# Projected queries and keys kept whole in their slot, split in place during the value products; every row maximum taken for both heads at once

## The reference

```python
h = _ln(x, g1, be1)
x = _attn(h, h, Wq1, Wk1, Wv1, Wo1, bo1) + x          # self-attention, 1024 keys
h = _ln(x, g2, be2)
x = _attn(h, context, Wq2, Wk2, Wv2, Wo2, bo2) + x    # attention to 64 context rows
h = _ln(x, g3, be3)
y = h @ Wp + bp
x = y[..., :1024] * gelu(y[..., 1024:]) @ W2 + b2 + x

def _attn(x, ctx, Wq, Wk, Wv, Wo, bo):                # 16 heads of 64
    sim = einsum('bihd,bjhd->bhij', q, k) * 64 ** -0.5
    return einsum('bhij,bjhd->bihd', softmax(sim), v) @ Wo + bo
```

## Time and profile before

| what | us |
|---|---|
| median of 3 runs | 1986.89 (1986.82 to 1987.51) |
| the profiled execution, its own time | 1987.43 |
| its span in the profile | 1985.6 |
| PE busy | 1973.7 (99%) |
| POOL busy | 1490.1 (75%) |
| DVE busy | 1396.3 (70%) |
| ACT busy | 1143.7 (58%) |
| granted TensorE clock | 1.00 |

### The profile page before, as it was taken

How to read it: one execution, slowest core, us unless ns; L and a number is a source line. 1 busy time by engine, 2 the same in 40 slices (tenths; PEclk the granted TensorE clock), 3 DMA queues, 4 the chain that set the end, 5 groups by cost and what they waited for, 6 DMA issues and landing times.

```text
span 1985.6 us, 32165 instructions
## 1 busy us (share of the span) xinstructions
PE 1973.7 (99%) x12056; PEld 1353.4 (68%) x12056; DVE 1396.3 (70%) x2437; ACT 1143.7 (58%) x2042; POOL 1490.1 (75%) x800
## 2 busy tenths in 40 slices
PE   9999999999999999999999999999999999999999
PEld 7655655666565656755655666565569999888888
DVE  6688687666868886587787666867867888744443
ACT  6665576555656666465666555656756766533332
POOL 3699899989999998899899899989996665200000
PEclk9999999999999999999999999999999999999999
DMA  7201000001000000010000001000030420000000
GB/s 256 107 28 43 6 6 17 6 27 49 17 12 6 17 6 27 8 58 6 6 22 6 27 1 54 7 27 1 23 106 22 150 65 1 1 22 33 33 11 32
DMA packets 48956, 67.15 MB, mean 34 GB/s; under 512 B 6177, under 2 KB 42145, under 8 KB 46753
## 3 DMA queue, kind: packets, MB, share of 16 engines
q1 hardware_dynamic: 48800, 65.10, 10.2%
HBM read 45.17 MB, written 19.92 MB: 33 GB/s over the span
## 4 chain that ended last, share of the span: by engine, by line
PE 94%; POOL 3%; DVE 2%; issue 1%; ACT 1%; POOLq 0%; DVEq 0%
PE score L576 22%; PE score L555 19%; PE score L702 9%; PE attn_project L511 8%; PE attn_project L687 5%; PE attn_project L716 5%; PE score L523 5%; PE score L657 4%; PE score L625 3%; PE first_score L537 3%; PE attn_project L537 3%; PE score L561 3%; POOL acc L1545 2%; PE first_score L671 1%; PE first_score L587 1%
## 5 line engine op out<-in xcount | busy, mean ns | idle before, releaser
L1545 POOL TENSOR_TENSOR acc<-acc,pT 128x1024 f32<-128x1024 f32 x384 | 918.1, 2391 | 54.7 <-POOL acc L1545 1.4
L1289 ACT ACTIVATE pT<-score 128x1024 f32<-128x1024 f32 x512 | 507.7, 1027 | 107.5 <-PE score L561 70.4
L555 PE MATMUL score<-qk 64*128 64x512 f32 x3072 | 466.5, 405 | 0.9 <-ACT pT L1289 0.4
L576 PE MATMUL score<-pT,vT 128*64 128x512 f32 x1952 | 432.3, 595 | 0.0
L555 PEld LDWEIGHTS score<-qk 64*128 64x128 f32 x3072 | 269.0, 184 | 123.3 <-ACT pT L1289 82.0
L914 DVE TENSOR_REDUCE nmax<-attn_project 128x2 f32<-128x1024 f32 x256 | 312.7, 1221 | 7.3 <-PE attn_project L537 3.9
L576 PEld LDWEIGHTS score<-pT,vT 128*64 128x64 f32 x1952 | 134.8, 137 | 265.8 <-issue 243.8
L914 DVE TENSOR_REDUCE nmax<-first_score 128x2 f32<-128x1024 f32 x201 | 245.1, 1219 | 0.2 <-issue 0.2
L511 PE MATMUL attn_project<-hT,wqk 128*128 128x512 f32 x738 | 185.9, 400 | 0.0
L702 PE MATMUL score<-hT,wp 128*128 128x512 f32 x768 | 183.7, 395 | 0.0
L1542 POOL TENSOR_TENSOR acc<-pT 128x1024 f32<-128x1024 f32 x64 | 153.0, 2390 | 27.5 <-ACT pT L1289 27.5
(11 more groups left out here) (202 smaller groups left out, 3127.5 us busy)
## 6 DMA issues: line engine op xcount, KB each, us to landing
xres<-x_middle SPq DMA_DIRECT2D x10, 512.0 KB, 3.6
raw_qk<-in_L_xattn_Wq SPq DMA_DIRECT2D x32, 128.0 KB, 2.2
raw_qk<-in_L_xattn_Wk SPq DMA_DIRECT2D x32, 128.0 KB, 2.4
raw_v<-in_L_xattn_Wv SPq DMA_DIRECT2D x8, 512.0 KB, 4.7
keys_all<-keys SPq DMA_DIRECT2D x1, 4096.0 KB, 13.1
values_all<-values SPq DMA_DIRECT2D x1, 4096.0 KB, 13.3
out_x<-xres SPq DMA_DIRECT2D x7, 512.0 KB, 2.9
xres<-in_x SPq DMA_DIRECT2D x3, 1024.0 KB, 5.7
```

The source lines that it names most:

```text
L555: last = e.matmul(bank, key_part(P, h, r, jt), queries1[P % 2][r, w, c * BANK:(c + 1) * BANK], start=(fresh and part == 0), stop=(not fres ...
L576: last = e.matmul(banks[bank][head * DH:(head + 1) * DH, :], vT[:, v_slot(D, jt), c0:c0 + DH], pT[:, jt, head, :], start=(jt == 0), stop=( ...
L1289: e.activation(pT[:, jt].rearrange("p h n -> p (h n)"), SC[R % 2][:, :], ACT.Exp).then_inc(s.exponential, 1)
L1545: e.tensor_tensor(total, total, pT[:, jt], ALU.add).then_inc(s.probs_added, 1)
```

## The change

- ScalarE copies the projected keys and the scaled queries in full precision into the places that their lo parts will take (`keys_whole`, `queries_whole`: the same bytes as keys lo and queries lo), and rounds the keys for the first scores. With this the bank is free (`qk_kept`).
- The rest is done one pass later, during the value products, from SBUF to SBUF: VectorE changes the keys in place and takes one lo half (`change_keys`), ScalarE rounds the changed half and the queries, VectorE takes the other lo half and the queries' lo part (`split_qk`).
- `row_max_of`, `early_max` and `keys_full` are gone; all row maxima are taken for both heads at once.
- TensorE's two first scores of round 0 come after the scores of that round and not ahead of them.

```diff
-        keys_full = sb("keys_full", [PART, BANK // 2])
+        queries_whole = [tile[:, N:2 * N] for tile in (qk0_whole, qk1_whole)]
+        keys_whole = [tile[:, 2 * N:3 * N].rearrange("p (c n) -> p c n", c=CHUNKS) for tile in (qk0_whole, qk1_whole)]
...
+        def units(C):
+            after, c = C // CHUNKS + 1 + C % CHUNKS, C % CHUNKS
+            return [(after, 1 - c), (after, 3 - c)] if after < B * PAIRS else []
...
 # tensor
-                free[bank] = ((s.split_lo, qk_of[P, u]),)
+                free[bank] = ((s.qk_kept, qk_of[P, u]),)
...
             for C in range(NC):
-                if C + 1 < NC:
-                    for head in range(2):
-                        first_score(*next_part(C + 1, 0), head)
                 for jt in range(TILES):
...
-                    if C + 1 < NC and jt:
+                    if C + 1 < NC:
                         for head in range(2):
                             first_score(*next_part(C + 1, jt), head)
...
 # vector
-            def change_keys(P, u, bank, coming=None):
-                n, later = keys_of[P, u], banks[bank][:, PAIR:]
-                need.wait_ge(s.keys_rounded, n)
-                need.wait_ge(s.keys_copied, n)
-                e.tensor_tensor(keys_lo[P % 2][:, u, 0:PAIR], banks[bank][:, 0:PAIR],
+            def change_keys(P, u):
+                whole = keys_whole[P % 2][:, u, :]
+                need.wait_ge(s.qk_kept, qk_of[P, u])
+                e.tensor_tensor(whole[:, PAIR:], whole[:, PAIR:], whole[:, 0:PAIR], ALU.subtract
+                                ).then_inc(s.keys_changed, 1)
+                need.wait_ge(s.keys_changed, keys_of[P, u])
+                e.tensor_tensor(keys_lo[P % 2][:, u, 0:PAIR], whole[:, 0:PAIR],
                                 keys_hi[P % 2][:, u, PAIR:2 * PAIR].bitcast(F32), ALU.subtract)
-                e.tensor_tensor(later, later, keys_full[:, :], ALU.subtract).then_inc(s.keys_changed, 1)
-                if coming:
-                    row_max_of(coming, 0)
...
+            def split_qk(P, u):
                 need.wait_ge(s.split_hi, qk_of[P, u])
...
+                    whole, lo = (part[P % 2][:, u, PAIR:] for part in (keys_whole, keys_lo))
+                    hi = keys_hi[P % 2][:, u, 0:PAIR]
                 else:
-                    split_queries(P, u, bank)
+                    span = slice((u - 2) * BANK, (u - 1) * BANK)
+                    whole, (hi, lo) = queries_whole[P % 2][:, span], (queries1[P % 2][:, w, span] for w in range(2))
+                e.tensor_tensor(lo, whole, hi.bitcast(F32), ALU.subtract).then_inc(s.split_lo, 1)
...
                     for i in range(TILES):
-                        if i == 0 and early_max(C + 1):
-                            row_max_of(C + 1, 1)
-                        else:
-                            row_max(*next_part(C + 1, i))
+                        row_max(*next_part(C + 1, i))
                     gather_max(C + 1)
                     turn_max(C + 1)
+                for unit in units(C - 1)[0:1] if C else ():
+                    change_keys(*unit)
...
                 if C:
                     fold_sums(C - 1)
...
+                for unit in units(C - 1) if C else ():
+                    split_qk(*unit)
...
-                whole_array(slot(C), C + 2 if early_max(C + 2) else None)
+                whole_array(slot(C))
...
 # scalar
+            def keep_qk(P, u, bank="PJ"):
...
+                if u < 2:
+                    e.copy(keys_whole[P % 2][:, u, :], banks[bank])
+                    e.copy(keys_hi[P % 2][:, u, PAIR:], banks[bank]).then_inc(s.qk_kept, 1)
+                else:
+                    e.activation(queries_whole[P % 2][:, (u - 2) * BANK:(u - 1) * BANK], banks[bank], ACT.Copy, scale=SCALE
+                                 ).then_inc(s.qk_kept, 1)
+
+            def split_qk(P, u):
...
+                e.copy(hi, whole).then_inc(s.split_hi, 1)
...
                 if C + 1 < NC:
                     make_shift(C + 1)
+                for unit in units(C - 1) if C else ():
+                    split_qk(*unit)
                 write_oT(C)
                 whole_array(slot(C))
```

More of the change, by code:

```diff
@@ L351, in slot @@
             jobs += [(*job, through[i % len(through)]) for i, job in enumerate(between)]
[L352 to L356, removed]
+            jobs += [("qk", *unit, bank) for unit, bank in zip(units(C), ("PV", "PJ"))]
             return jobs + [("out1", *tile, through[i % len(through)]) for i, tile in enumerate(out1_tiles(C))]
-        def early_max(C):
-            return 2 <= C < NC and (C - 2) // CHUNKS + 1 + C % CHUNKS < B * PAIRS and not out1_tiles(C - 2)
+        def units(C):
+            after, c = C // CHUNKS + 1 + C % CHUNKS, C % CHUNKS
+            return [(after, 1 - c), (after, 3 - c)] if after < B * PAIRS else []
         def out1_tiles(C):
@@ L532, in first_score @@
                 need.wait_ge(s.split_hi, qk_of[P, 2 + c])
-                need.wait_ge(s.keys_rounded, keys_of[P, half])
+                need.wait_ge(s.qk_kept, qk_of[P, half])
                 bank_free(bank)
@@ L897, in split_queries @@
-            def split_queries(P, u, bank):
-                span = slice((u - 2) * BANK, (u - 1) * BANK)
-                need.wait_ge(s.split_hi, qk_of[P, u])
-                hi, lo = (queries1[P % 2][:, w, span] for w in range(2))
-                e.scalar_tensor_tensor(lo, banks[bank], SCALE, hi.bitcast(F32), ALU.mult, ALU.subtract
-                                       ).then_inc(s.split_lo, 1)
-            def split_qk(P, u, bank="PJ", coming=None):
                 if u < 2:
-                    change_keys(P, u, bank, coming)
-                else:
-                    split_queries(P, u, bank)
+                    need.wait_ge(s.keys_changed, keys_of[P, u])
@@ L1072, in _ @@
             turn_norm((1, 1))
-            for u, bank in zip((0, 2, 1), CTX_BANKS):
-                split_qk(0, u, bank)
+            for u in range(CHUNKS):
+                change_keys(0, u)
             for i in range(TILES):
@@ L1078, in _ @@
             turn_max(0)
-            split_qk(0, 3, "PJ")
-            split_qk(1, 0, "S1a")
-            split_qk(1, 2, "S1b")
+            for u in (0, 2, 1, 3):
+                split_qk(0, u)
+            change_keys(1, 0)
+            split_qk(1, 0)
+            split_qk(1, 2)
             for C in range(NC):
@@ L1346, in whole_array @@
                     if job[0] == "qk":
-                        split_qk(*job[1:])
+                        keep_qk(*job[1:])
                     elif job[0] == "v":
@@ L1422, in _ @@
             for u, bank in zip((0, 2, 1), CTX_BANKS):
-                split_qk(0, u, bank)
+                keep_qk(0, u, bank)
+            for u in (0, 2, 1):
+                split_qk(0, u)
             for n in range(PAIRS // 2 * (B // 2)):
```

46 lines of the change are left out of this document (19 added, 27 removed).

## The result

The changed kernel takes 2140.22 us (median of 4 runs, 2139.57 to 2143.51) against 1986.86 for the kernel before: a ratio of 1.0775, 95% interval 1.0756 to 1.0793, 153 us slower. The forecast was 2096 us.

The account below looks back on a forecast made before the run. TensorE, 99% busy, bounds the kernel before; VectorE becomes the bound. Losses of 51, 27, 16 and 15 us sum to 109, making the span 2094.6 and the execution, 1.8 above, 2096 us; range 2030 to 2165.

Parts of the forecast that it names:

- The turns with GpSimd: VectorE's four SBUF subtractions a pass wait for ends of GpSimd additions; a plain pass takes 21.15 us against 19.56.
- Rival 1: Between keys' change and first lo half VectorE keeps its turn; only TensorE's gain is left, 1977 us; chance 0.08.
- Rival 2: VectorE's subtractions just miss GpSimd's ends, a wait of about 2.2 us; 2191 us; chance 0.10.
- rival 3: Half of the subtractions' waits vanish in gaps of GpSimd; plain pass about 20.2 us, 2027 us in all; chance 0.14.
- Plain passes, 32 x 1.6 = 51 us: 32 passes without projections, "ln" or statistics each lose 1.6 us to the subtractions' waits, 51 us.
- Statistics, 9 x 3.0 = 27 us: Nine passes with statistics between fold and second lo half just miss a GpSimd end; 22.55 us each, 27 us lost.
- "ln" passes, 7 x 2.3 = 16 us: Seven passes with 2.2 us more VectorE work, against 21.06 us before, lose 2.3 us each, 16 us.
- Value and output projections, 13 x 1.15 = 15 us: In 13 passes further TensorE work hides all but the wait for the fold; 1.15 us each, 15 us.
- TensorE's order, 0.16 us a pass: First scores of round 0 behind its scores let the exponential come earlier; alone 10 us gained over 62 passes.
- What would show it: Signs: VectorE busy 250 us more, TensorE about 94%, waits at fold and first scores, plain passes 21 to 21.5.

Follow-up runs that it names:

- wo1_on_pool: Changed kernel, with the output weights' subtraction of passes 1 to 4 made by GpSimd behind its additions, not by VectorE: 2129.34 us, ratio 1.0717.
- warm: Changed kernel plus unread 128x128 matmuls on TensorE where it stood idle 2.4 us or more in passes with a low clock: 2129.72 us, ratio 1.0718.
- fold_first: Changed kernel, with the fold of the row sums moved ahead of the keys' change on VectorE: 2191.8 us, ratio 1.1034.
- one_reduce: Changed kernel, its four SBUF subtractions a pass replaced by same-size VectorE reductions over a length-one axis (one SBUF input): 1977.4 us, ratio 0.995.
- order_joint: Kernel before, with only TensorE's first scores of round 0 behind the scores and all row maxima joint: 1985.61 us, ratio 0.9993.
- adds_small: Changed kernel, with six of GpSimd's seven additions a pass cut from 512 to 16 numbers a head: 1979.82 us, ratio 0.9962.
- one_input: Changed kernel, its four subtractions a pass replaced by scalar operations on one SBUF tensor and two per-partition scalars: 2121.8 us, ratio 1.0678.

## Why the prediction was right, and where it was off

The direction, the mechanism and the place were right; the size was 44 us too small (2096 for 2140, inside the range). The missed terms come to more than 44: the statistics passes were priced 9.5 us too dear in all, which hid part of the others by luck.

- **The turns with GpSimd.** The forecast, for the plain pass, had the keys' change at 0.27 past an end, the first half at the next end, the second half and the queries' at one each. The timeline after shows this in order: the 256-wide ones end 0.28 to 0.29 us behind an end (forecast 0.27), the queries' part 0.55 (forecast 0.53). Rival 1, by which VectorE keeps its turn between the change and the half, fell: the half takes 2335 ns on average. Rival 2 (ends just missed) and rival 3 (half of them vanish) fell as a rule for all passes: the plain pass of 21.15 came out as 21.08 to 21.16 in 13 of the 22 plain intervals. Rival 3's way is seen in two: in intervals 32 and 48 GpSimd has short splits of oT among its additions, the first half took 0.56 and 0.84 us for 2.47, and they lost only 0.17.
- **Plain passes, 32 x 1.6 = 51 us.** The 22 truly plain intervals gave 37.8 (1.7 each). Of the other ten that I had put under this price, one lies at the end (interval 61, which lost 5.6 at a clock of 0.86) and nine were not plain. Three of these, and the ninth of the statistics passes, are the opening's four intervals. They gave 21.2 instead of 7.8: I had read the output weights' subtraction in the earlier trace rows as evidence and did not see that it stays in the changed kernel, one more turn ahead of the fold. wo1_on_pool took 10.9 us of it back. In three GpSimd first splits the value weights, in the three behind these it adds biases; I had asked only whether GpSimd catches up, not when its ends come. The pass that I read as the plain one was itself of the first kind: its late addition at 658.21 was no backlog but stood behind that split. Six such intervals gave 19.9 instead of 9.6. One of the first kind:

```profile
723.95 2.39 POOL L1494 TENSOR_TENSOR wv<-raw_v,wv 128x1024 fp32r<-128x1024 f32 x1
726.30 2.39 POOL L1540 TENSOR_TENSOR acc<-pT 128x1024 f32<-128x1024 f32 x1
728.84 12.39 POOL L1543 TENSOR_TENSOR acc<-acc,pT 128x1024 f32<-128x1024 f32 x5
...
734.03 2.50 DVE L884 TENSOR_TENSOR qk_whole<-qk_whole 128x256 f32<-128x256 f32 x1
...
740.11 4.18 DVE L899 TENSOR_TENSOR qk<-qk_whole,qk 128x256 fp32r<-128x256 f32 x2
740.24 0.63 PE L588 MATMUL first_score<-folded,quads 128*128 128x32 f32 x2 [2.83 <-DVE folded L929]
740.68 4.39 PE L512 MATMUL attn_project<-hT,wqk 128*128 128x512 f32 x12
```

  The first addition starts 8.78 us after the sum matmul of 717.52; in interval 8 that is 7.16. So the keys' change meets almost a whole addition (2.50 for 0.92): rival 2, true in a few passes. TensorE waits 2.83 us, and the projections take 4.39 instead of 3.02, which is the lower clock (0.50 in the two microseconds from 740.5) and falls into the next interval.
- **Statistics, 9 x 3.0 = 27 us.** Too dear. Eight intervals lost 14.5 (24 forecast) and the ninth lies in the opening. They lost 1.4 to 2.0, one 2.7, as plain ones do. I had them just miss an end of GpSimd's (17.45 for 17.40). They don't: in the interval that ends at 220.26 the fold starts at 218.97, two statistics follow, and the last subtraction ends at 224.37, 5.40 us after the fold's start; without statistics 293.03 to 298.42 are 5.39. A difference of 0.05 us between two sums of durations was no ground for 1.4 us a pass.
- **"ln" passes, 7 x 2.3 = 16 us.** The term most wrong: 36.2. I counted VectorE's 2.2 us of hT work but not who needs it, and in four of the seven intervals that work is 3.0 us (two operations of 0.82, two of 0.69). The scores of the next pass take the banks that the turned hT stands in, so TensorE itself waits for VectorE's last hT part:

```profile
366.05 0.52 DVE L937 RECIPROCAL rsum<-first_score 64x16 f32<-64x16 f32 x2
...
369.66 0.69 DVE L852 TENSOR_TENSOR hT<-score,hT 128x512 fp32r<-128x512 f32 x1
370.40 0.96 PE L556 MATMUL score<-qk 64*128 64x512 f32 x5 [3.85 <-DVE hT L852]
```

  Before, it ended at 349.01, 4.75 us after the sum matmul of 344.26, and 4.75 us after that of 323.20 too. In the changed kernel it ends in this interval at 370.35, 8.31 us after the sum matmul of 362.04, behind two subtractions that end at 366.13. The clock then falls (0.50 from 372 to 374), and VectorE, for whom this is the start of the pass, waits for the slow first scores. No run took the bank wait away by itself, so how the loss splits is open in general. Three of these intervals (13, 29, 45) give a bound: in warm, with the clock at 1.00, they still lost 3.9 us of the 5.2 to 5.9.
- **Value and output projections, 13 x 1.15 = 15 us.** 17.3 measured, nine of the thirteen at 1.1 to 1.4, the others at 0.5 to 2.7 and evened out by luck; fold_first brought exactly this loss to nothing.
- **TensorE's order, 0.16 us a pass, "alone 10 us".** The size is right inside the change (one_reduce is 9.5 below before in all) and wrong alone (order_joint, 1.3): the row maxima, not only the exponential, must come earlier too.
- **The clock.** The sum had no term for it. Before, it is 1.00; after, 0.981 over the span, and warm got 10.5 us back. My own waits were at 1.3 us, behind which it did not fall; those that the missed terms made were longer, and behind most of these it fell.
- **What would show it.** Busy time of VectorE 250 us or more up (318), TensorE at 94%, the wait of 1 us for the fold, the wait at the first scores, plain passes at 21 to 21.5: as listed. "Those with statistics longest" was wrong; the "ln" passes are.

The Trainium skill (SBUF — State Buffer, "SBUF: two separate sides") says that VectorE contends with GpSimd for the shared pair of ports in two cases: with two SBUF inputs, and in a mode that uses two ports. My prediction took up only the first. The runs agree for two inputs (adds_small, one_reduce). The scalar form of one_input, which has one SBUF tensor, waited as well, 1703 ns for 256 numbers; that fits the second case, but no trace names the mode.

## What to carry to other kernels

Before work is moved from PSUM operands to SBUF operands, look at what GpSimd does at that time and at the form of each VectorE instruction. Here a two-input or scalar operation on SBUF beside GpSimd's two-input operations mostly lasted until the end of the current one, whatever its size (1.1 to 2.6 us on average), and a reduction (404 and 677 ns) or an operation with a PSUM operand (684 ns) did not. Put such operations behind everything that another engine waits for, one at a time and with other work between them, and count each as one GpSimd operation. When a forecast makes another engine the bound, go through every kind of pass: what else the two engines do ahead of the contended operations, which shifts the ends that they meet, and who waits for each of their results. Here that, and the clock behind the longer waits, was the missing part of the loss, somewhat under a third of it.

## What the runs showed of the hardware that I had not expected

- A VectorE scalar operation on fp32 in SBUF takes turns with GpSimd like a two-input one: 256 numbers in 1105 and 1703 ns on average. It ends 0.15 us after GpSimd's end (256 numbers), the two-input form 0.28 us, in the two plain passes above.
- A reduction over SBUF of the same sizes takes 404 and 677 ns beside the same additions.
- The turns are one-sided: VectorE's busy time rose by 318 us, GpSimd's by 24 (1490.1 to 1513.8).
- The lower granted clock followed waits of TensorE of 2.83, 3.85 and 3.98 us; twelve projection matmuls then took 4.39 and 4.45 us instead of 3.02. Behind waits of 1.27 us it stayed at 1.00. In between it did either: it fell behind 1.71 and 1.73 us, and stayed behind 2.85.
